# Edge convolution on one core: VectorE makes the comparison arrays of the next step behind the copy of column numbers instead of at the start of that step

## The chip, the cores and the metric

The kernel runs on one core of one Trainium2 chip. The metric is the device time of one execution in microseconds (us). The engines are TensorE (PE; its weight loads are shown apart as PEld), VectorE (DVE), ScalarE (ACT), GpSimd (POOL) and SyncE (SP), which only issues DMAs here. Each works through its own instructions in order, and they wait for each other by semaphores.

## The reference, cut to what matters

The whole block is a graph network layer over 6250 nodes and 100000 edges, an attention mixer and a mixture of experts. The change touches one stage, the edge convolution:

```python
# x[src]: 256 wide; edge_attr: 64 wide; dst is sorted
msg = jax.nn.relu(x[src] + edge_attr @ We + be)
aggr = jax.ops.segment_sum(msg, dst, num_segments=N)
z = (1.0 + GINE_EPS) * x + aggr
```

In the same stage the kernel also counts, for a later stage, how many of 131072 other edges end at each node. That count uses one-hot products too.

## The kernel before

`gine_windows` is the stage. The edges are cut into 98 steps (`S1`) of 8 blocks (`B`) of 128 edges. Buffers alternate by `q`, the parity of the step `k = 2i + q`, and a step has two halves `h` of four blocks. Since `dst` is sorted, the edges of a step end in a window of 128 nodes; `rel` holds each edge's place in the window. One step is made of:

- POOL, `gather` (L421): eight indirect DMAs of 128 rows of 256 numbers, `xg[q]`, by the column numbers in `gidx[q]`.
- SP (L400): one DMA of edge attributes `eaT[q]`.
- PE, `project` (L456): `ps_e[h] = eaT @ We`, four blocks in each half.
- DVE (L588), twice: `msg[q, h] = ps_e[h] + xg[q, h]`. ACT then does the relu in place (L506).
- DVE, the comparison arrays: `inwin[q]` (L576, one-hot of `rel` in the window), and for the count `hot_hi[q]` (L581) and `hot_lo[q]` (L583). All three compare with the numbers 0 to 127 in `ps_io`.
- PE: count products `ps_cnt += hot_lo.T @ hot_hi` (L463, eleven small bf16 products), and window sums `ps_a[q] = inwin.T @ msg` (L473, eight products).
- ACT, `save_sums` (L498): copies the sums of step k-1 to `nsum`. PE turns them (`turn_sums`, L444) in the middle of step k, and DVE adds the turned sums into `zT` (`add_window`, L569).
- DVE, `stage_next` (L562): copies the column numbers for step k+2 into `gidx[q]`, which starts POOL's next gather for that buffer. In even steps DVE also takes one `bn_stats` (L596).

PE's step k runs in this order: wait for `hot_lo[k]`, count (L463); wait for the first half of the messages of step k, project the first half of step k+1 (L456); wait for its relu, window sums of the first half (L473); turn the sums of step k-1 (L444); project the second half of step k+1; window sums of the second half. ACT's step k is: wait for the window sums of step k-1 and save them, then the two relus. DVE's step k before is: comparison arrays of step k, two message additions, column numbers, wait for turned sums (`s_nt`), `add_window`, `bn_stats`. The order on each engine is the order of the written code; no planner is involved.

In the print below, `s_am[q]` counts finished window sums, `s_cnt[q]` finished counts, `s_nt` turned sums, `s_sum` message halves, `s_e[q]` projected halves and `s_g[q][h]` gathered halves.

Of the kernel before, what the change touches and what calls it, by code (L numbers as in the profile page):

```python
# [13 lines left out]
ALU = mybir.AluOpType  # L14
# [12 lines left out]
B = 8  # L27
# [297 lines left out]
def gine_windows(nc, A, M):  # L325
# [5 lines left out]
    with ExitStack() as ctx:  # L331
# [59 lines left out]
        with nc.Block() as block:  # L391
# [122 lines left out]
            def _(dve):  # L514
# [43 lines left out]
                def stage_next(i, q):  # L558

                    for h in range(2):  # L560
                        dve.wait_ge(s_g[q][h], i * 64 + 64)
                    nc.vector.tensor_copy(gidx[:, q, :], M["src1"][:, bass.ds((i * 2 + q) * B + 2 * B, B)]).then_inc(s_gi, 1)  # L562

                def add_window(k, q):

                    at = nc.values_load(basei[0:1, k], engines=[dve.engine], min_val=0, max_val=N - 1,
                                        skip_runtime_bounds_check_because="VectorE clamped it to these bounds")
                    here = M["zT"][:, :, bass.ds(at, P)]
                    nc.vector.tensor_tensor(here, ps_a[:, q, D:2 * D].rearrange("p (c n) -> p c n", c=KD), here, ALU.add).then_inc(s_agg, 1)  # L569

                with dve.Fori(0, S1 // 2) as i:
                    for q in range(2):
                        k = 2 * i + q

                        dve.wait_ge(s_am[q], i + q)
                        nc.vector.tensor_tensor(inwin[:, q, :, :], ps_io[0:W1E, None, :].broadcast_to([W1E, B, P]),  # L576
                                                rel[:, bass.ds(k * B, B)][:, :, None].broadcast_to([W1E, B, P]), ALU.is_equal).then_inc(s_win[q], 1)

                        dve.wait_ge(s_cnt[q], i)
                        cols = bass.ds(k * CB, CB)  # L580
                        nc.vector.tensor_tensor(hot_hi[:, q, :, :], ps_io[:, None, 0:NHI].broadcast_to([P, CB, NHI]),  # L581
                                                M["hi"][:, cols][:, :, None].broadcast_to([P, CB, NHI]), ALU.is_equal).then_inc(s_hi, 1)
                        nc.vector.tensor_tensor(hot_lo[:, q, :, :], ps_io[:, None, :].broadcast_to([P, CB, P]),  # L583
                                                M["lo"][:, cols][:, :, None].broadcast_to([P, CB, P]), ALU.is_equal).then_inc(s_hot, 1)
                        for h in range(2):
                            dve.wait_ge(s_e[q], i * 2 + (h + 1))
                            dve.wait_ge(s_g[q][h], i * 64 + 64)
                            nc.vector.tensor_tensor(msg[:, q, h * HB:(h + 1) * HB, :].rearrange("p b d -> p (b d)"), ps_e[h][:, :],  # L588
                                                    xg[:, q, h * HB:(h + 1) * HB, :].rearrange("p b d -> p (b d)"), ALU.add).then_inc(s_sum, 1)
                        dve.wait_ge(s_sum, 2 * k + 2)  # L590
                        stage_next(i, q)
                        dve.wait_ge(s_nt, k + 1)
                        dve.wait_ge(s_agg, k)
                        add_window(bass.ds(k, 1), 1 - q)
                        if q == 0:
                            nc.vector.bn_stats(M["bst"][:, bass.ds(i, 1), :].rearrange("p t s -> p (t s)"),  # L596
                                               M["xn"][:, bass.ds(i, 1), :].rearrange("p t d -> p (t d)")).then_inc(s_stat, 1)
                dve.wait_ge(s_nt, S1 + 1)
                dve.wait_ge(s_agg, S1)
                add_window(slice(S1, S1 + 1), 1)  # L600
# [1874 lines left out]
```

## Time and profile before

| | us |
|---|---|
| median of 3 runs | 3788.47 (3782.95 to 3798.07) |
| the profiled execution, its own time | 3779.81 |
| its span, first to last instruction | 3777.8 |
| starts of `hot_lo` in the first and the last of the 98 steps | 81.7 and 1352.1 |

The profiled execution lies 8.7 us under the median. A line of the profile names the kernel's line, the engine, the operation, what it writes and reads, and behind the bar or in brackets how long the engine stood idle just before it and which instruction ended that. "remote" and "issue" mean that no instruction in the trace is seen to end the wait. One matrix product of f32 numbers is two records of the trace, so the four products of a half step are x8. A granted clock of 1.00 is 2.4 GHz and 0.50 is 1.2 GHz.

### The profile page before, as it was taken

The page shows a single profiled execution, that of the slowest core. Times are in us where ns is not written, and L with a number is a line of the kernel's source. Part 1 is how long each engine was busy: PE and PEld are TensorE (multiplying, and loading weights), DVE is VectorE, ACT ScalarE, POOL GpSimd, SP SyncE. Part 2 cuts the span into 40 slices and gives each one's busy share as a digit, 9 for nine tenths or more (in the row PEclk, how much of TensorE's full clock was granted, in tenths as well). Part 3 has the DMA queues.
Part 4 walks back from the last instruction along what each step waited for, and adds up shares of the span by engine and source line. Part 5 has one row for each costly group of instructions (what it writes and reads, how often), then busy time and mean ns, then how long its engine had stood idle before and what let it go on. Part 6 is the DMA issues. An engine that isn't in the chain of part 4 may idle for free. (4 is left out here: it accounts for less than half of the span.)

```text
span 3777.8 us, 34904 instructions
## 1 busy us (share of the span) xinstructions
PE 2708.7 (72%) x10528; PEld 1927.9 (51%) x10528; DVE 1621.8 (43%) x3135; ACT 692.7 (18%) x1082; POOL 1704.2 (45%) x1746
## 2 busy tenths in 40 slices
PE   3887888788788777799998865766766766765007
PEld 2666666666666655666665542433434433434006
DVE  6444555455454467666778960000000000001784
ACT  1111111111111123223332220111101101101005
POOL 1565656556565510022221216666666666662211
PEclk8777777777777779999999986878878877877558
DMA  7433333333333332200000013222222212213415
GB/s 259 131 105 91 106 101 106 99 100 104 97 108 93 99 99 74 68 23 23 23 23 12 9 12 70 37 36 37 37 36 37 37 31 37 41 30 109 145 59 229
DMA packets 215309, 280.82 MB, mean 74 GB/s; under 512 B 95634, under 2 KB 166312, under 8 KB 213706
## 3 DMA queue, kind: packets, MB, share of 16 engines
q0 software_dynamic: 68416, 133.35, 14.6%
q1 hardware_dynamic: 105994, 108.62, 9.3%
q10 hardware_dynamic: 40832, 38.01, 3.2%
q8 instruction: 35, 0.57, 0.1%
q14 instruction: 32, 0.26, 0.0%
HBM read 215.36 MB, written 64.48 MB: 74 GB/s over the span
## 5 line engine op out<-in xcount | busy, mean ns | idle before, releaser
L421 POOL DMA_INDIRECT xg<-xn_dram,gidx x784 | 743.9, 949 | 526.2 <-DVE gidx L562 283.2
L1962 POOL DMA_INDIRECT er<-row_dram,gi x784 | 739.9, 944 | 430.7 <-issue 411.9
L2023 PE MATMUL ps_en<-ew,hid 128*128 128x256 f32 x1568 | 404.5, 404 | 216.6 <-issue 213.4
L2095 DVE TENSOR_TENSOR eo<-ps_en,eb_r 128x1024 f32<-128x1024 f32 (+1 forms) x52 | 60.5, 1163 | 1157.7 <-remote 851.5
L2013 PE MATMUL ps_em<-zT_all,ew 128*128 (+2 forms) x832 | 420.4, 646 | 190.9 <-issue 123.7
L456 PE MATMUL ps_e<-we,eaT 65*128 65x256 f32 x1568 | 507.2, 480 | 69.3 <-issue 56.2
L473 PE MATMUL ps_a<-arena 128*128 128x256 f32 x1568 | 522.1, 491 | 34.6 <-ACT arena L506 26.4
L2023 PEld LDWEIGHTS ps_en<-ew,hid 128*128 128x128 f32 x1568 | 314.7, 202 | 311.6 <-issue 271.6
L473 PEld LDWEIGHTS ps_a<-arena 128*128 128x128 f32 x1568 | 399.0, 256 | 134.2 <-ACT arena L506 34.8
L456 PEld LDWEIGHTS ps_e<-we,eaT 65*128 65x128 f32 x1568 | 356.8, 239 | 138.8 <-issue 74.0
L2013 PEld LDWEIGHTS ps_em<-zT_all,ew 128*128 128x128 f32 x832 | 172.9, 215 | 419.6 <-issue 386.8
L2060 ACT ACTIVATE hid<-ps_em,eb 128x512 f32<-128x512 f32 (+1 forms) x208 | 130.4, 663 | 1087.2 <-DVE eo L2095 403.6
L569 DVE TENSOR_TENSOR zT_all<-ps_a,zT_all 128x256 f32 x99 | 42.1, 425 | 626.2 <-PE ps_a L444 358.5
L1514 POOL TENSOR_SCALAR hg<-hg,mv,rs 128x256 f32<-128x256 f32 x49 | 72.5, 1490 | 509.3 <-DVE rs L1320 462.7
L2268 PE MATMUL ps_c<-eo,dgm 128*128 128x256 f32 x294 | 69.4, 394 | 228.3 <-ACT dgm L2224 224.1
L588 DVE TENSOR_TENSOR arena<-ps_e,xg 128x1024 f32<-128x1024 f32 x196 | 230.0, 1216 | 0.0
L498 ACT ACTIVATE nsum<-ps_a 128x256 f32<-128x256 f32 x99 | 38.0, 384 | 1025.0 <-remote 792.0
L506 ACT ACTIVATE arena<-arena 128x1024 f32<-128x1024 f32 x196 | 198.5, 1049 | 49.9 <-DVE arena L588 30.0
L1613 PE MATMUL ps_m<-zT,arena 128*128 128x512 f32 (+1 forms) x416 | 183.8, 599 | 19.8 <-ACT zT L1682 19.4
L2268 PEld LDWEIGHTS ps_c<-eo,dgm 128*128 128x128 f32 x294 | 56.8, 197 | 240.9 <-issue 233.2
L1622 PE MATMUL ps_n<-arena,hid 128*128 128x256 f32 x784 | 173.9, 379 | 0.8 <-ACT hid L1688 0.8
L583 DVE TENSOR_TENSOR hot_lo<-ps_io,lo 128x1408 bf16<-128x1408 f32 x98 | 158.3, 1616 | 0.0
(291 smaller groups left out, 2877.0 us busy)
## 6 DMA issues: line engine op xcount, KB each, us to landing
eaT<-in_eaT SPq DMA_DIRECT2D x98, 256.0 KB
eo_dram<-eo ACTq DMA_DIRECT2D x48, 512.0 KB
eo<-eo_dram SPq DMA_DIRECT2D x12, 2048.0 KB
xg<-xn_dram,gidx POOLq DMA_INDIRECT x784
er<-row_dram,gi POOLq DMA_INDIRECT x784
xm<-xm_dram SPq DMA_DIRECT2D x24, 512.0 KB
erow<-arena ACTq DMA_DIRECT2D x1, 10240.0 KB
erow<-er SPq DMA_DIRECT2D x196, 40.0 KB
```

The lines of the kernel that those rows point to most:

```text
L421: pool.indirect_dma_start(xg[:, q, b, :], None, M["xn_dram"], bass.IndirectOffsetOnAxis(ap=gidx[:, q, b:b + 1], axis=0)).then_inc(s_g[q][b ...
L456: t = pe.matmul(ps_e[h][:, b * D:(b + 1) * D], eaT[:, q, h * HB + b, :], we[:, :], start=True, stop=True)
L473: t = pe.matmul(ps_a[:, q, 0:D], inwin[:, q, b, :], msg[:, q, b, :], start=(b == 0), stop=(b == B - 1), skip_group_check=True)
L506: nc.scalar.activation(msg[:, q, h * HB:(h + 1) * HB, :], msg[:, q, h * HB:(h + 1) * HB, :], ACT.Relu).then_inc(s_msg, 1)
L583: nc.vector.tensor_tensor(hot_lo[:, q, :, :], ps_io[:, None, :].broadcast_to([P, CB, P]), M["lo"][:, cols][:, :, None].broadcast_to([P, CB ...
L588: nc.vector.tensor_tensor(msg[:, q, h * HB:(h + 1) * HB, :].rearrange("p b d -> p (b d)"), ps_e[h][:, :], xg[:, q, h * HB:(h + 1) * HB, :] ...
L1613: m = pe.matmul(ps_m[c % 2][:, 0:w], mw1[:, k, c * P:(c + 1) * P], zT[:, k, 0:w], start=(k == 0), stop=(k == KD - 1))
L1622: m = pe.matmul(ps_n[:, t, :], hid[:, c, t * P:(t + 1) * P], mw2[:, c, :], start=(c == 0), stop=(c == KH - 1))
L1962: pool.indirect_dma_start(er[:, r, b, :], None, M["row_dram"], bass.IndirectOffsetOnAxis(ap=gi[:, r, b:b + 1], axis=0)).then_inc(s_get[r], 16)
L2013: m = pe.matmul(ps_m[c][:, 0:w], w1[:, e, k, c * P:(c + 1) * P], xT[:, k, at], start=(k == 0), stop=(k == KD - 1))
L2023: m = pe.matmul(ps_n[b][:, t, :], hid[:, b, c, t * P:(t + 1) * P], w2[:, e, c, :], start=(c == 0), stop=(c == KE - 1))
L2060: nc.scalar.activation(hid[:, b, c, 0:w], ps_m[c][:, 0:w], ACT.Gelu, bias=b1[:, e * KE + c:e * KE + c + 1]).then_inc(s_ge, 1)
```

## The change

The three comparisons become a function `compare(k, q, n)`. It is called once for step 0 ahead of the loop. Inside step k it is called for step k+1, with the other buffer, right behind `stage_next` and ahead of the wait for turned sums. To leave it out in the last step, the loop runs over `LASTI` (48) pairs, and the last two steps are written out behind it. The waits keep their meaning: `inwin` of step k+1 may be written once the window sums of step k-1 are done, and the `hot` arrays once the count of step k-1 is done. No instruction on another engine changes.

```diff
-                with dve.Fori(0, S1 // 2) as i:
+                def compare(k, q, n):
+
+                    dve.wait_ge(s_am[q], n + q)
+                    nc.vector.tensor_tensor(inwin[:, q, :, :], ps_io[0:W1E, None, :].broadcast_to([W1E, B, P]),
+                                            rel[:, bass.ds(k * B, B)][:, :, None].broadcast_to([W1E, B, P]), ALU.is_equal).then_inc(s_win[q], 1)
+
+                    dve.wait_ge(s_cnt[q], n)
...
+                def step(i, q, more):
+                    k = 2 * i + q
...
+                    dve.wait_ge(s_sum, 2 * k + 2)
+                    stage_next(i, q)
+                    if more:
+                        compare(k + 1, 1 - q, i + q)
+                    dve.wait_ge(s_nt, k + 1)
+                    dve.wait_ge(s_agg, k)
+                    add_window(bass.ds(k, 1), 1 - q)
...
+                compare(0, 0, 0)
+                with dve.Fori(0, LASTI) as i:
                     for q in range(2):
-                        dve.wait_ge(s_am[q], i + q)
...
-                        dve.wait_ge(s_sum, 2 * k + 2)
-                        stage_next(i, q)
-                        dve.wait_ge(s_nt, k + 1)
-                        dve.wait_ge(s_agg, k)
-                        add_window(bass.ds(k, 1), 1 - q)
...
+                        step(i, q, True)
+                step(LASTI, 0, True)
+                step(LASTI, 1, False)
```

On DVE, the second half of the loop's body (q = 1) reads as follows before. `arena<-ps_io,rel` is `inwin`, `arena<-ps_e,xg` a message half, and L566 is the wait for turned sums; `s_am11` is `s_am[1]`, `s_cnt11` is `s_cnt[1]`, and `s_e11` is `s_e[1]`.

```order
L576 ISA [waits s_am11]
L576 TENSOR_TENSOR arena<-ps_io,rel 128x1024
L581 ISA [waits s_cnt11]
L581 TENSOR_TENSOR hot_hi<-ps_io,hi 128x704
L583 REGISTER_ALU
L583 TENSOR_TENSOR hot_lo<-ps_io,lo 128x1408
L588 TENSOR_TENSOR arena<-ps_e,xg 128x1024 [waits s_std,s_e11]
L588 TENSOR_TENSOR arena<-ps_e,xg 128x1024 [waits s_xn,s_e11]
L590 ISA
L562 ISA [waits s_xn,s_std,s_sum1]
L562 COPY gidx<-src 128x8
L566 ISA [waits s_agg1,s_nt1]
```

Now the three comparisons for q = 1 stand in the first half of the body (q = 0), between the column numbers and the wait for turned sums (`s_nt1`, L566):

```order
L562 COPY gidx<-src 128x8
L573 REGISTER_ALU
L574 ISA [waits s_am11]
L574 TENSOR_TENSOR arena<-ps_io,rel 128x1024
L579 ISA [waits s_cnt11]
L579 TENSOR_TENSOR hot_hi<-ps_io,hi 128x704
L581 REGISTER_ALU
L581 TENSOR_TENSOR hot_lo<-ps_io,lo 128x1408
L566 ISA [waits s_agg1,s_nt1]
L566 TENSOR_LOAD basei
L569 ISA
L569 TENSOR_TENSOR zT_all<-ps_a,zT_all 128x2x128
```

The comparisons moved ahead of the addition L569. The message halves of q = 1 now follow the addition (and, in this half, `bn_stats`) directly; nothing was added to or taken from the body. L574, L579, L581 and L589 are the old L576, L581, L583 and L588.

## Rows read from the trace of the kernel before

**Rows 1.** The page: busy us (share of the span), instructions.

```profile
PE 2708.7 (72%) x10528; PEld 1927.9 (51%) x10528; DVE 1621.8 (43%) x3135; ACT 692.7 (18%) x1082; POOL 1704.2 (45%) x1746
```

**Rows 2.** The line of `hot_lo`: count, duration in ns, first and last start.

```profile
L583 DVE TENSOR_TENSOR hot_lo<-ps_io,lo x98: 1612/1616/1618, 81.7 to 1352.1; 128x1408 bf16<-128x1408 f32 x98
```

**Rows 3.** Groups by line over 82:1353: busy, mean ns | idle before, releasers.

```profile
L421 POOL DMA_INDIRECT xg<-xn_dram,gidx x773 | 731.0, 946 | 522.4 <-DVE gidx L562 283.2 <-issue 239.2
...
L456 PE MATMUL ps_e<-we,eaT 65*128 65x256 f32 x1552 | 500.0, 478 | 62.4 <-issue 56.2 <-DVE arena L588 6.2
...
L588 DVE TENSOR_TENSOR arena<-ps_e,xg 128x1024 f32<-128x1024 f32 x194 | 227.7, 1216 | 0.0
...
L463 PE MATMUL ps_cnt<-hot_hi,hot_lo 128*128 128x64 bf16 x1067 | 49.0, 196 | 131.9 <-DVE hot_lo L583 114.4 <-issue 17.5
```

**Rows 4.** Timeline of PE, one step: start, us, instruction, [idle before, releaser].

```profile
1003.11 3.56 PE L456 MATMUL ps_e<-we,eaT 65*128 65x256 f32 x8 [0.63 <-issue]
1006.47 3.62 PE L473 MATMUL ps_a<-arena 128*128 128x256 f32 x8
...
1010.25 1.89 PE L456 MATMUL ps_e<-we,eaT 65*128 65x256 f32 x8
1011.98 1.89 PE L473 MATMUL ps_a<-arena 128*128 128x256 f32 x8
1015.24 0.49 PE L463 MATMUL ps_cnt<-hot_hi,hot_lo 128*128 128x64 bf16 x11 [1.37 <-DVE hot_lo L583]
1016.37 3.18 PE L456 MATMUL ps_e<-we,eaT 65*128 65x256 f32 x8 [0.63 <-issue]
```

**Rows 5.** Timeline of DVE and ACT over the same step.

```profile
1004.34 0.17 DVE L562 COPY gidx<-src 128x8 int32 x1
1010.97 0.43 DVE L569 TENSOR_TENSOR zT_all<-ps_a,zT_all 128x256 f32 x1 [6.46 <-issue]
...
1011.65 1.21 DVE L576 TENSOR_TENSOR arena<-ps_io,rel 128x1024 f32<-128x1024 f32 x1
...
1013.57 1.62 DVE L583 TENSOR_TENSOR hot_lo<-ps_io,lo 128x1408 bf16<-128x1408 f32 x1
...
1016.70 0.39 ACT L498 ACTIVATE nsum<-ps_a 128x256 f32<-128x256 f32 x1 [10.77 <-remote]
1016.98 1.99 ACT L506 ACTIVATE arena<-arena 128x1024 f32<-128x1024 f32 x2
```

**Rows 6.** Windows: PE, PEld, DVE, ACT, POOL busy; granted clock, DMA share, GB/s.

```profile
82.00:1353.00 1271.00, 1043.71 (x4365) 817.58 (x4365) 634.16 (x729) 226.37 (x292) 731.40 (x774) 0.77 0.37 105
1003.40:1010.10 6.70, 6.70 (x18) 5.11 (x18) 0.96 (x2) 2.27 (x3) 3.78 (x4) 0.50 0.21 61
1010.20:1017.00 6.80, 4.80 (x32) 3.85 (x31) 6.03 (x7) 0.30 (x2) 3.79 (x4) 1.00 0.47 135
...
1770.00:1950.00 180.00, 170.22 (x753) 123.62 (x752) 131.34 (x367) 55.10 (x77) 43.10 (x24) 1.00 0.07 24
```

**Rows 7.** Timeline of POOL, where one gather follows the other without a wait.

```profile
961.36 0.94 POOL L421 DMA_INDIRECT xg<-xn_dram,gidx  x1 [1.86 <-DVE gidx L562]
...
971.36 0.95 POOL L421 DMA_INDIRECT xg<-xn_dram,gidx  x1 [0.30 <-issue]
```

**Rows 8.** Timeline of PE, a short step and the one behind it.

```profile
958.06 0.49 PE L463 MATMUL ps_cnt<-hot_hi,hot_lo 128*128 128x64 bf16 x11 [1.37 <-DVE hot_lo L583]
...
961.01 1.89 PE L473 MATMUL ps_a<-arena 128*128 128x256 f32 x8
...
967.82 0.49 PE L463 MATMUL ps_cnt<-hot_hi,hot_lo 128*128 128x64 bf16 x11 [1.23 <-DVE hot_lo L583]
...
978.55 0.70 PE L473 MATMUL ps_a<-arena 128*128 128x256 f32 x2 [0.34 <-issue]
...
989.15 0.77 PE L463 MATMUL ps_cnt<-hot_hi,hot_lo 128*128 128x64 bf16 x11 [4.18 <-DVE hot_lo L583]
```

**Rows 9.** The same view: the last such step.

```profile
1244.68 0.49 PE L463 MATMUL ps_cnt<-hot_hi,hot_lo 128*128 128x64 bf16 x11 [1.48 <-issue]
...
1265.45 0.49 PE L463 MATMUL ps_cnt<-hot_hi,hot_lo 128*128 128x64 bf16 x11 [2.60 <-DVE hot_lo L583]
```

More of the change, by code:

```diff
@@ L569, in add_window @@
                     nc.vector.tensor_tensor(here, ps_a[:, q, D:2 * D].rearrange("p (c n) -> p c n", c=KD), here, ALU.add).then_inc(s_agg, 1)
-                with dve.Fori(0, S1 // 2) as i:
-                    for q in range(2):
-                        k = 2 * i + q
-                        dve.wait_ge(s_am[q], i + q)
[L576 to L589, printed above, removed]
-                        dve.wait_ge(s_sum, 2 * k + 2)
-                        stage_next(i, q)
-                        dve.wait_ge(s_nt, k + 1)
-                        dve.wait_ge(s_agg, k)
-                        add_window(bass.ds(k, 1), 1 - q)
-                        if q == 0:
-                            nc.vector.bn_stats(M["bst"][:, bass.ds(i, 1), :].rearrange("p t s -> p (t s)"),
-                                               M["xn"][:, bass.ds(i, 1), :].rearrange("p t d -> p (t d)")).then_inc(s_stat, 1)
@@ new lines, in compare @@
+                def compare(k, q, n):
[3 more added lines that the diff above has]
+                    dve.wait_ge(s_cnt[q], n)
+                    cols = bass.ds(k * CB, CB)
+                    nc.vector.tensor_tensor(hot_hi[:, q, :, :], ps_io[:, None, 0:NHI].broadcast_to([P, CB, NHI]),
+                                            M["hi"][:, cols][:, :, None].broadcast_to([P, CB, NHI]), ALU.is_equal).then_inc(s_hi, 1)
+                    nc.vector.tensor_tensor(hot_lo[:, q, :, :], ps_io[:, None, :].broadcast_to([P, CB, P]),
+                                            M["lo"][:, cols][:, :, None].broadcast_to([P, CB, P]), ALU.is_equal).then_inc(s_hot, 1)
@@ new lines, in step @@
+                def step(i, q, more):
+                    k = 2 * i + q
+                    for h in range(2):
+                        dve.wait_ge(s_e[q], i * 2 + (h + 1))
+                        dve.wait_ge(s_g[q][h], i * 64 + 64)
+                        nc.vector.tensor_tensor(msg[:, q, h * HB:(h + 1) * HB, :].rearrange("p b d -> p (b d)"), ps_e[h][:, :],
+                                                xg[:, q, h * HB:(h + 1) * HB, :].rearrange("p b d -> p (b d)"), ALU.add).then_inc(s_sum, 1)
+                    dve.wait_ge(s_sum, 2 * k + 2)
[5 more added lines that the diff above has]
+                    add_window(bass.ds(k, 1), 1 - q)
+                    if q == 0:
+                        nc.vector.bn_stats(M["bst"][:, bass.ds(i, 1), :].rearrange("p t s -> p (t s)"),
+                                           M["xn"][:, bass.ds(i, 1), :].rearrange("p t d -> p (t d)")).then_inc(s_stat, 1)
```

## The prediction

> **What bounds the kernel now.** The page's shares say little: PE is busy 72% of the span and no engine is full [rows 1], because stages with different limits are added up. The change touches one stage, so I first fixed that stage by the line of `hot_lo`, which runs once per step: 98 starts from 81.7 to 1352.1 us [rows 2]. That is 1270.4 us for 97 intervals, 13.10 us a step. All that follows is made against this number; outside these 1270 us nothing changes.
>
> Then I read one step in the timeline of PE and asked where it stands still. From one count (L463) to the next there are only two holes: 1.37 us until VectorE's `hot_lo` is there, and 0.63 us between the count and the first projection [rows 4]. The second hole ends by nothing that the trace names, but the code says what it is: the projection waits for the first message half, and VectorE makes that half directly behind `hot_lo`. So both holes are one fact: VectorE starts the comparisons too late. The timeline of VectorE shows why. It finishes the column numbers at 1004.5, stands idle 6.46 us until the turned sums are there, adds them at 1010.97, and only then starts `inwin` at 1011.65, ending `hot_lo` at 1015.19 [rows 5]; PE starts the count 0.05 us later [rows 4]. VectorE is on the path for 3.5 us of comparisons that it could have made in its idle 6.46.
>
> Over the stage, the grouped lines give the same two holes: PE idle 131.9 us before L463 and 62.4 us before L456 [rows 3], together 194.3 us, or 2.0 us a step.
>
> Two more facts matter. The granted clock in the stage is 0.77 on average, and it alternates: 0.50 (1.2 GHz) from 1003.4 to 1010.1, where PE had come out of the two holes, then 1.00 (2.4 GHz) [rows 6]. Eight records take 3.4 us at the lower level and 1.7 us at the upper (1003.11 to 1006.47 against 1010.25 to 1011.98) [rows 4]. And POOL is not far away: where nothing holds it, eight gathers take 10.00 us (961.36 to 971.36, without a break between two groups) [rows 7].
>
> **The change part by part.**
>
> *Comparisons into the idle time.* VectorE's three comparisons cost 3.54 us from the start of the first to the end of the last (1011.65 to 1015.19) [rows 5]. They move into an idle stretch of 6.46 us, so in such a step they cost nothing there. Their own waits are for window sums and count of step k-1. The sums of the step before were seen by ScalarE at 1016.70, 2.8 us after PE's last product of them ended (1011.98 + 1.89 = 13.87) [rows 4, 5]. VectorE comes to them behind the column numbers, one step (13.26 us, from 1003.11 to 1016.37) after 1004.34, at 1017.6, so in this step that wait is over. If the cover were gone, the comparisons would delay `add_window` and the message halves behind it, at most by 3.54 us a step.
>
> *What is queued behind them.* On VectorE `add_window` and the next two message halves stand behind the comparisons. The column numbers stand ahead of them, so POOL's start is not delayed. ScalarE, SyncE and POOL keep their order.
>
> *What goes on PE.* `hot_lo` of step k+1 is ready a whole half step early, so the 1.37 us go. The first message half of step k+1 now comes right behind `add_window` (the comparisons themselves started 0.68 us behind its start, 1010.97 to 1011.65 [rows 5]), not behind 3.5 us of comparisons: with its 1.2 us (L588, mean 1216 ns [rows 3]) it is done 1.9 us after the addition starts, about 1012.9 by this step's times, while PE still works until 13.87. So the 0.63 us go as well. Term: 131.9 + 62.4 = 194.3 us [rows 3]. I take off 4 us for the first steps, where other things start up: 190 us.
>
> *What is late next.* ScalarE. Its relu of step k stands behind the copy of the sums of step k-1. Here copy and relu run from 1016.70; the first relu ends at 1016.98 + about 1.0 = 18.0 [rows 5]. PE's window sums of that step can't start before. If the sums are still seen 2.8 us late when PE no longer pauses, PE could start them at 18.0 instead of 19.35 (16.37 + 3.0), and the gain in this step is 1.3 us, not 2.0. In the step at full clock (958.06 to 967.82, 9.8 us) PE started its sums at 961.01 [rows 8], and nothing would be won. With three quarters of the steps like the first kind, this end is 0.75 x 97 x 1.3 = 95 us. These rows leave two reasons for the delay open: the sums may be seen late because PE pauses right behind them (then the delay goes with the pause), or for a reason of their own. The other groups of products, which PE follows up at once, let their readers start within 0.7 us (PE turned from turned sums to the projection at 1010.25, and `add_window` ran at 1010.97 [rows 4, 5]), so I lean to the first and keep 95 us as the low end.
>
> *The clock.* At the other end, if the holes are what lowers the clock, it stays up without them. In a stage without such holes, 1770 to 1950, PE is busy 170 of 180 us at 1.00 [rows 6]. Then PE needs 9.8 - 2.0 = 7.8 us a step and POOL becomes the bound at 10.0 us: POOL's whole wait for column numbers, 283.2 us [rows 3], goes and no more.
> The Trainium skill, TensorE: Matmul & The Clock Gate, section "A second HAM failure mode: psum-queue depth-cycling", says that short idles between groups of matmuls are enough to make the clock oscillate between half and full rate. The trace agrees in that the clock falls with holes of 1.37 and 0.63 us in the step and stays up where there are none. By that rule the time would be that of the POOL rival below.
> I don't take this end as the forecast: a PE that waits for POOL 2.2 us in 10.0 has a hole of the same size as now, and the clock would fall again.
>
> *Loop.* Two steps are written out behind the loop; the body has as many instructions as before. Nothing in the sum.
>
> **Sum.** Profiled execution 3779.8 - 190 = 3589.8. The median of the runs lies 8.7 us over the profiled execution, so 3598 us by the median. A step takes 13.10 - 1.96 = 11.1 us.
>
> **The rivals.**
>
> *POOL becomes the bound.* The clock rises, PE falls under 10.0 us a step, the gathers follow each other without a wait. Gain 283 us: 3505 us. For it: the holes and the clock go together [rows 4, 6], and gathers did run without a break [rows 7]. Against it: the new hole behind POOL.
>
> *The relu behind the copy.* The 95 us case above: 3693 us, steps of 12.1 us. For it: the copy is seen to wait 2.8 us after PE's last product. Against it: that product is one that PE pauses behind.
>
> *Slow stretches.* This one ends slower. From 978.55 on PE's products come with short unexplained idles where they otherwise follow each other every 0.22 us, and the step from 967.82 to 989.15 takes 21.3 us [rows 8]. It comes directly behind the short step of 9.8 us. There are six steps of 18.9 to 21.3 us in the stage, the last from 1244.68 to 1265.45 [rows 9], and five of them stand directly behind the only five steps under 10.3 us. If short steps bring on such a stretch (both PE and POOL are then at their densest), a kernel with steps of 10 us meets it again and again: two steps of 10.0 and one of 21.3 make 13.77 on average, 97 x 0.67 = 65 us slower: 3853 us. It decides from 13.1 us a step on; at 11 us a step that needs 25 more stretches of 8 us than now, every fourth step. Against it: most steps will not be as short as 10 us, and the dense stage at 1770 to 1950 runs at full rate with PE busier than here (but POOL and DMA nearly quiet, DMA share 0.07 against 0.37) [rows 6].
>
> *The change does not do what it says.* VectorE might reach the comparisons too late or be held in them by the late sums, so that `hot_lo` is no earlier. That needs the idle 6.46 us [rows 5] to be gone; at most the gain would be near nothing: 3788 us.
>
> **How the numbers follow.** Forecast (both holes go, the clock shares about as now, steps 10.7 to 11.5 us, 3560 to 3640 us): 0.37. POOL bound, or near it (3500 to 3560): 0.26. Relu behind the copy, or some more slow stretches that eat part of the gain (3640 to 3720): 0.25. Little left (3720 to 3769): 0.03. No change: 0.04. Slower: 0.05. The range reaches from the POOL end to most of the relu end: 3500 to 3700 us. A change of 0.5% is 19 us, about what a measurement of this kernel can tell from none. Faster by more than that 0.91, within it 0.04, slower 0.05.
>
> **What would show it.** Right: in the grouped lines PE's idle before L463 and before L456 falls from 194 us to under 20, the steps (98 starts of `hot_lo`) take about 11.1 us, VectorE's idle moves from before `add_window` to before the message halves or shrinks, and POOL's wait for column numbers falls by about the gain, to some 90 us. The POOL rival: that wait is near nothing, and steps are 10.0 us. The relu rival: PE's idle before L473, released by ScalarE's relu, grows from 24 us to 100. The slow-stretch rival: more than 20 steps above 18 us. The clock: under 0.77 or at it for the forecast, well above for the POOL rival. Wrong altogether would be an idle of PE before L463 that stays above 100 us.

## The result, and the profile after the change

The changed kernel takes 3864.19 us in the median of 4 runs (3841.99 to 3869.21), the kernel before 3791.55 us (4 runs, 3782.95 to 3798.07): a ratio of 1.0182, 95% interval 1.0143 to 1.022. The forecast was 3598 us with a range of 3500 to 3700. Both the number and the direction were wrong here; on another kind of chip, met later, the direction was right. The profiled execution of after is 3841.99 us, its span 3840.0.

First the line of `hot_lo`, as [rows 2], then the groups by line over 82:1420, as [rows 3] (busy us, mean ns | idle before, releasers), and the same stretch in the windows view, as [rows 6]:

```profile
L581 DVE TENSOR_TENSOR hot_lo<-ps_io,lo x98: 1615/1616/1617, 81.4 to 1412.6; 128x1408 bf16<-128x1408 f32 x98
```

```profile
L421 POOL DMA_INDIRECT xg<-xn_dram,gidx x773 | 730.9, 946 | 589.8 <-DVE gidx L562 358.8 <-issue 231.0
L473 PE MATMUL ps_a<-arena 128*128 128x256 f32 x1556 | 525.2, 481 | 234.8 <-issue 185.7 <-ACT arena L506 46.0
L456 PE MATMUL ps_e<-we,eaT 65*128 65x256 f32 x1552 | 448.8, 430 | 91.3 <-issue 52.0 <-DVE arena L589 38.5
...
L574 DVE TENSOR_TENSOR arena<-ps_io,rel 128x1024 f32<-128x1024 f32 x97 | 118.8, 1225 | 167.9 <-remote 150.0 <-issue 14.2 <-PE ps_a L473 3.4
...
L463 PE MATMUL ps_cnt<-hot_hi,hot_lo 128*128 128x64 bf16 x1078 | 59.2, 208 | 18.4 <-issue 16.5 <-DVE hot_lo L581 1.6
```

```profile
82.00:1420.00 1338.00, 994.06 (x4380) 765.43 (x4381) 644.27 (x732) 228.81 (x294) 731.29 (x774) 0.78 0.35 100
```

The stage grew from 1270.4 to 1331.2 us, 13.72 us a step. That is the whole loss of the profiled execution (62 us). The comparisons did what they should: PE's idle before the count fell from 131.9 to 18.4 us. But PE now stands 234.8 us before the window sums (L473). Before, that line read:

```profile
L473 PE MATMUL ps_a<-arena 128*128 128x256 f32 x1552 | 515.6, 490 | 32.8 <-ACT arena L506 24.5 <-issue 7.9
```

I split PE's idle in the stage by whether it stands ahead of the first product of a group or between two products of one group, which should follow each other without a gap:

| PE in the stage, us | before | after |
|---|---|---|
| ahead of a count (L463) or a projection (L456) | 131.9 + 60.5 | 3.9 + 44.6 |
| ahead of window sums (L473) | 25.8 | 167.9 |
| inside a group of products | 8.9 | 126.8 |
| busy | 1043.4 | 987.9 |

Each column adds up to the length of the stage. So the two holes lost 144 us, and as much (142) came back as one ahead of the window sums. On top come 118 us inside the groups, and PE's busy time fell by 55. The sum is the stage's 61 us.

The timeline of PE in one stretch shows both new losses (start, us, instruction, [idle before, releaser]):

```profile
556.14 1.89 PE L473 MATMUL ps_a<-arena 128*128 128x256 f32 x8
557.87 0.48 PE L463 MATMUL ps_cnt<-hot_hi,hot_lo 128*128 128x64 bf16 x11
558.19 1.97 PE L456 MATMUL ps_e<-we,eaT 65*128 65x256 f32 x8
565.27 3.78 PE L473 MATMUL ps_a<-arena 128*128 128x256 f32 x8 [5.11 <-issue]
...
590.24 0.38 PE L456 MATMUL ps_e<-we,eaT 65*128 65x256 f32 x1 [0.77 <-issue]
591.64 0.59 PE L456 MATMUL ps_e<-we,eaT 65*128 65x256 f32 x1 [1.03 <-issue]
...
593.06 0.58 PE L473 MATMUL ps_a<-arena 128*128 128x256 f32 x1 [0.40 <-issue]
594.46 1.22 PE L473 MATMUL ps_a<-arena 128*128 128x256 f32 x2 [0.82 <-issue]
...
599.41 0.59 PE L473 MATMUL ps_a<-arena 128*128 128x256 f32 x1 [0.82 <-issue]
600.12 0.77 PE L463 MATMUL ps_cnt<-hot_hi,hot_lo 128*128 128x64 bf16 x11
```

ScalarE and VectorE at the same places, in the same view:

```profile
563.89 0.38 ACT L498 ACTIVATE nsum<-ps_a 128x256 f32<-128x256 f32 x1 [14.24 <-remote]
564.17 1.99 ACT L506 ACTIVATE arena<-arena 128x1024 f32<-128x1024 f32 x2
```

```profile
558.16 0.17 DVE L562 COPY gidx<-src 128x8 int32 x1 [0.17 <-issue]
564.01 1.23 DVE L574 TENSOR_TENSOR arena<-ps_io,rel 128x1024 f32<-128x1024 f32 x1 [5.67 <-remote]
...
576.27 0.17 DVE L562 COPY gidx<-src 128x8 int32 x1
...
582.74 0.17 DVE L562 COPY gidx<-src 128x8 int32 x1 [0.17 <-issue]
```

**Late signals.** The window sums ended at 558.03 (556.14 + 1.89). ScalarE's copy and VectorE's `inwin` both wait for exactly these, and both start 5.9 us later, at 563.89 and 564.01. The relu stands behind the copy, so PE's next window sums stand still until 565.27. It is the signal that comes late and not its readers: of the 54 copies of after that start over 0.5 us late, 51 have an update of their semaphore in the trace, each time 0.02 us before the copy starts. (The profile models the ends of PE's products, so the last product itself may have ended later than 558.03.) And "issue" at 565.27 doesn't mean that PE waited for nothing: the relu ended at 565.22, but the trace has no record of its update of the semaphore, so the profile could not name it.

**Slow products.** From 590.24 on most of PE's records, or pairs of them, begin about 0.7 or 1.4 us apart (590.24, 591.64, 593.06, 594.46), where they begin 0.22 us apart otherwise at the full clock; it ends before 600.12. And POOL, which began its gathers again at 577.23:

```profile
568.42 0.95 POOL L421 DMA_INDIRECT xg<-xn_dram,gidx  x1 [0.30 <-issue]
577.23 0.94 POOL L421 DMA_INDIRECT xg<-xn_dram,gidx  x1 [7.86 <-DVE gidx L562]
...
595.99 0.95 POOL L421 DMA_INDIRECT xg<-xn_dram,gidx  x1 [0.30 <-issue]
604.94 0.94 POOL L421 DMA_INDIRECT xg<-xn_dram,gidx  x1 [8.00 <-DVE gidx L562]
```

Sixteen gathers run without a pause from 577.23 to 596.94, since the two copies of column numbers came only 6.47 us apart (576.27 and 582.74), less than eight gathers take. The slow products begin 13.0 us into this run and end some 2.5 us behind it. In before nearly all runs have eight gathers.

Steps by the starts of `hot_lo`: before has 7 over 18 us (one of them the first, at start-up) and 5 under 10.3; after has 21 over 18 (one of them at start-up) and 23 under 10.3, and 20 of those 23 are followed directly by one over 18.

### The profile page after: what moved, and what is told of

Read it like the earlier page. It is cut to its first block and busy times, and to the rows that moved or that the text cites. A ratio compares the mean times of both kernels' runs of the same rounds, so it can differ in the third digit from the quotient of the medians.

```text
span 3840.0 us, 34837 instructions
## 1 busy us (share of the span) xinstructions
PE 2653.0 (69%) x10528; PEld 1873.4 (49%) x10528; DVE 1629.4 (42%) x3135; ACT 692.1 (18%) x1082; POOL 1704.0 (44%) x1746
## 5 line engine op out<-in xcount | busy, mean ns | idle before, releaser
L421 POOL DMA_INDIRECT xg<-xn_dram,gidx x784 | 743.8, 949 | 593.6 <-DVE gidx L562 358.8
L473 PE MATMUL ps_a<-arena 128*128 128x256 f32 x1568 | 528.0, 480 | 234.8 <-issue 185.7
L2105 DVE TENSOR_TENSOR eo<-ps_en,eb_r 128x1024 f32<-128x1024 f32 (+1 forms) x52 | 60.5, 1163 | 1158.1 <-remote 938.3
L473 PEld LDWEIGHTS ps_a<-arena 128*128 128x128 f32 x1568 | 369.0, 240 | 368.1 <-issue 257.0
L456 PE MATMUL ps_e<-we,eaT 65*128 65x256 f32 x1568 | 456.0, 432 | 98.1 <-issue 52.0
L456 PEld LDWEIGHTS ps_e<-we,eaT 65*128 65x128 f32 x1568 | 323.2, 217 | 153.0 <-issue 67.0
L569 DVE TENSOR_TENSOR zT_all<-ps_a,zT_all 128x256 f32 x99 | 42.0, 424 | 501.1 <-remote 396.9
L589 DVE TENSOR_TENSOR arena<-ps_e,xg 128x1024 f32<-128x1024 f32 x196 | 230.6, 1216 | 13.5 <-remote 9.1
L574 DVE TENSOR_TENSOR arena<-ps_io,rel 128x1024 f32<-128x1024 f32 x98 | 120.0, 1225 | 167.9 <-remote 150.0
```

The costliest lines, as they stand in the source:

```text
L421: pool.indirect_dma_start(xg[:, q, b, :], None, M["xn_dram"], bass.IndirectOffsetOnAxis(ap=gidx[:, q, b:b + 1], axis=0)).then_inc(s_g[q][b ...
L456: t = pe.matmul(ps_e[h][:, b * D:(b + 1) * D], eaT[:, q, h * HB + b, :], we[:, :], start=True, stop=True)
L473: t = pe.matmul(ps_a[:, q, 0:D], inwin[:, q, b, :], msg[:, q, b, :], start=(b == 0), stop=(b == B - 1), skip_group_check=True)
```

## The experiments

A fact that came out between the experiments goes first, since every result hangs on it. **Chips differ.** On some chips the kernel before takes 3790 to 3800 us in the median; on others 3478 to 3490 us. On the first kind the profile has late signals and slow products, on the second it has neither, in any kernel. I call them the slower chips and the quicker chips; no chip is known to have been met twice, so whether this is the chip or its state at that time is open. Kernels are compared only with runs of before on the same chip.

The theories at the start: **A**, products that follow each other too densely make PE slow down; A1, what counts is the array's consumption, so zeros would help; A2, what counts is the rate of PE's instructions. **B**, gathers without a pause hold PE up. Later: **C**, the change is good by itself, and the loss comes from the slower chips; **D**, the new order on VectorE costs on any chip.

### Taking one load away: no gathers, zeros, half the sums

All three start from the changed kernel. Without gathers:

```diff
-                    for b in range(B):
-                        pool.indirect_dma_start(xg[:, q, b, :], None, M["xn_dram"],
-                                                bass.IndirectOffsetOnAxis(ap=gidx[:, q, b:b + 1], axis=0)).then_inc(s_g[q][b // HB], 16)
...
+                c.done(nc.vector.memset(xg[:, :, :, :], 0.5))
```

> The changed kernel without its 784 gathers in the edge convolution: xg is filled once with 0.5, VectorE waits for no gather, GpSimd only passes semaphores on; the sums are not the reference's. In the changed kernel 97 steps take 1331 us (13.7 us a step), with some 25 steps over 18 us in which TensorE's products come at 0.7 us and more apart. Theory A (TensorE itself: products without a pause at the full clock bring on the slow stretches): the slow stretches stay, since TensorE is as dense or denser, and steps stay well above 10 us on average, the whole at 3700 to 3850 us. Theory B (gathers that follow each other without a break, or their transfers, bring them on): no step over 15 us is left, TensorE bounds the stage at 7.8 to 8.5 us a step, and the whole takes 3791 - 97 x (13.1 - 8.2), about 3320 us.

Zeros in PE's products:

```diff
-                sp.dma_start(we[0:ED, :], A["We"]).then_inc(s_w, 16)
-                sp.dma_start(we[ED:ED + 1, :], mm(A["be"], 1)).then_inc(s_w, 16)
...
+                nc.vector.memset(we[:, :], 0.0).then_inc(s_w, 1)
...
-                                                xg[:, q, h * HB:(h + 1) * HB, :].rearrange("p b d -> p (b d)"), ALU.add).then_inc(s_sum, 1)
+                                                xg[:, q, h * HB:(h + 1) * HB, :].rearrange("p b d -> p (b d)"), ALU.mult).then_inc(s_sum, 1)
```

> The changed kernel with the same instructions and waits, but zeros run through TensorE in the edge convolution: the weights of the projection are zeroed instead of loaded, and the messages are ps_e times xg instead of ps_e plus xg, so all f32 products move zeros; the sums are not the reference's. Theory A1 (it is what the array consumes at full rate with real numbers, so the operands matter): no slow stretch is left, steps are 10.0 us, bound by the gathers, the stage takes about 980 us and the whole about 3864 - 350 = 3510 us. Theory A2 (it is the rate of TensorE's instructions, whatever they compute) and theory B (the gathers): nothing changes, the stage stays at 1331 us and the whole at 3840 to 3870 us.

Two window-sum products in each half instead of four:

```diff
-                        for b in range(h * HB, h * HB + HB):
+                        for b in range(h * HB, h * HB + 2):
```

> The changed kernel with half of the window sums left out: two products instead of four in each half step, all other work and all transfers as before; the sums are not the reference's. TensorE has 24 f32 records a step instead of 32, 5.8 us of work a step at the full clock. Theory A (TensorE's density): the slow stretches go or become rare (under 5), steps are near the gathers' 10.0 us and the stage near 1000 us, the whole about 3530 us. Theory B (gathers without a break): with steps of 10.0 us the gathers run without a break all the time, so there are as many slow stretches as in the changed kernel or more, the stage stays over 1250 us and the whole over 3790 us.

Measured: 3033.08, 3263.3 and 3261.36 us, where before takes 3477.96 on the same chip, with steps of 7.56, 10.01 and 10.00 us. It looked as if each of the three cured the stage. But in the stage of experts, which none of them touches, TensorE's products had also shrunk from 1196 us to some 699, so the chip was another one, and the experiments told nothing of the cause. What they do give is a bound. Without gathers PE alone needs 7.56 us a step at full clock:

```profile
L577 DVE TENSOR_TENSOR hot_lo<-ps_io,lo x98: 1611/1615/1617, 85.8 to 819.5; 128x1408 bf16<-128x1408 f32 x98
```

```profile
86.00:819.00 733.00, 730.04 (x4337) 635.03 (x4338) 638.46 (x726) 219.54 (x291) 0.00 (x0) 0.99 0.14 40
```

That is the line of `hot_lo` and the windows view of the repeat on a second quicker chip (3028.61 us, before 3490.12).

### The same kernels on a slower chip, and half of the change

> The changed kernel itself, beside the kernel before on the same chip. Where the kernel before takes about 3480 us (as it did beside the three runs without slow stretches) and not 3790 us, the slow stretches belong to the chip and not to the program. Theory C (the change is good by itself, and only a chip with slow stretches turns it into a loss): on a chip where before takes about 3480 us, the changed kernel has no step over 15 us, steps of 10.0 us bound by the gathers, and takes about 3265 us, ratio 0.94; on a chip where before takes about 3790 us, ratio 1.018 again with some 25 steps over 18 us. Theory D (the loss is in the order on VectorE, whatever the chip): the ratio is 1.00 or above on either chip.

> The kernel before, for its trace on the same chip. Theory C: on a chip that takes 3480 us for it, no step over 15 us in the edge convolution, steps of 12 to 13 us with the two holes of 1.37 and 0.63 us on TensorE, and none of the stretches in the expert stage in which products come at 0.7 us and more apart. If the chip takes 3790 us for it: some 6 steps over 18 us, as in the first trace. Theory D: TensorE's holes are the same on either chip.

The changed kernel repeats: 3843.34 us against 3799.03, ratio 1.013 (1.0064 to 1.0196), steps of 13.73 us, though only 15 of them are over 18 us and 20 under 10.3; before in one run 3800.89 us, 13.24 us a step. Two kernels make half of the change. One makes the `hot` arrays early and leaves `inwin` behind the addition, the other the reverse:

```diff
                     if more:
-                        compare(k + 1, 1 - q, i + q)
+                        counts(k + 1, 1 - q, i + q)
...
+                    if more:
+                        windows(k + 1, 1 - q, i + q)
```

> Half of the change: the two hot arrays of the count are made early, as in the changed kernel; inwin (1.1 us) is made behind the addition of turned sums, as before. TensorE's count then waits for nothing, but the first projection waits for the message half, which comes 1.1 us later than in the changed kernel. On a chip without slow stretches theory C expects steps between 10.0 and 10.5 us and 3265 to 3310 us. On a chip with them: TensorE pauses about 1 us a step, so there are fewer stretches than in the changed kernel (10 to 18 instead of 25), steps of 12.8 to 13.4 us and 3760 to 3830 us. Theory D: within 10 us of the changed kernel on either chip.

> The other half: inwin is made early, the two hot arrays (2.4 us) behind the addition, as before. TensorE's hole before the count shrinks from 1.37 to about 0.25 us and the 0.63 us behind it stay. On a chip without slow stretches theory C expects steps of 10.0 to 11.5 us and 3270 to 3400 us; on a chip with them about 12.5 to 13.2 us a step, 5 to 15 stretches and 3740 to 3800 us. Theory D: within 10 us of the changed kernel on either chip.

Measured: 3880.39 us, ratio 1.0236 (1.0167 to 1.0305), steps of 14.01 us; and 3862.34 us, ratio 1.0168 (1.0102 to 1.0235), 14.05 us in the profiled execution. Neither half is better than the whole, and both forecasts were missed: 22 and 30 steps over 18 us (with the start-up) instead of 10 to 18 and 5 to 15. With `inwin` late, PE waits 127.9 us for the message halves behind it; with the `hot` arrays late, PE's wait for them is back, at 170.4 us. But the slow products are in both. The loss does not belong to one of the three comparisons.

### Repeats that met quicker chips, and the comparison they made possible

The three kernels above ran again, and a version with less work for PE. It writes the relu's output and `inwin` in bf16, so that a window-sum product is one record instead of two:

```diff
-        inwin = M["arena"][0:W1E, 2 * B * D:2 * B * (D + P)].rearrange("p (q b n) -> p q b n", q=2, b=B)
+        inwin = M["arena"][0:W1E, 2 * B * D:2 * B * D + B * P].bitcast(BF16).rearrange("p (q b n) -> p q b n", q=2, b=B)
...
-                            t = pe.matmul(ps_a[:, q, 0:D], inwin[:, q, b, :], msg[:, q, b, :], start=(b == 0), stop=(b == B - 1), skip_group_check=True)
+                            t = pe.matmul(ps_a[:, q, 0:D], inwin[:, q, b, :], msg16(q, h)[:, b - h * HB, :], start=(b == 0), stop=(b == B - 1), skip_group_check=True)
...
-                            nc.scalar.activation(msg[:, q, h * HB:(h + 1) * HB, :], msg[:, q, h * HB:(h + 1) * HB, :], ACT.Relu).then_inc(s_msg, 1)
+                            nc.scalar.activation(msg16(q, h), msg[:, q, h * HB:(h + 1) * HB, :], ACT.Relu).then_inc(s_msg, 1)
```

> The kernel without gathers again (the changed kernel, xg filled once with 0.5, GpSimd passes semaphores on only), since the first time it ran on a chip that shows no slow stretch in any stage and so told nothing about their cause. On a chip where the kernel before takes about 3790 us: theory A (TensorE's own density brings on the stretches) expects TensorE to work almost without a pause and so to meet them more than ever, the stage at 1000 us or above against 733 us on the quiet chip. Theory B (gathers) expects steps of 7.6 us and no step over 12 us, the stage 733 us as on the quiet chip. On a quiet chip: again 733 us.

> The changed kernel, with the window sums in bf16: inwin is written as bf16 (zeros and ones, exact) and ScalarE's relu writes its result as bf16; all sums stay in f32. Eight short products take the place of sixteen f32 records a step, so TensorE's f32 work a step falls from 7.8 us at the full clock to about 4.5. This is the candidate that should beat both kernels if TensorE's density is what brings on the stretches. Theory A: no or under 5 steps over 18 us, steps of 10.0 us bound by the gathers, the stage at about 975 us on either chip; the whole at 3480 to 3520 us where before takes 3790, ratio 0.92 to 0.93, and at 3265 us where before takes 3480. Theory B (gathers without a break bring them on): the stage stays over 1250 us where before takes 3790, ratio 0.99 to 1.02.

These and the repeats of zeros and half sums (3259.72 and 3258.39 us) met a quicker chip: bf16 sums take 3257.92 us there, ratio 0.9344 (0.9292 to 0.9395), at 9.99 us a step. A second set brought what was missing, the changed kernel itself on a quicker chip:

> The changed kernel once more. Theory C on a chip where before takes about 3480 us: steps of 10.0 us, no step over 15 us but the first, the whole at 3265 us, ratio 0.94. On a chip where before takes about 3790 us: ratio 1.01 to 1.02 and 15 to 25 steps over 18 us, as twice before. Theory D (the order on VectorE costs time on any chip): a ratio of 1.00 or above on the quiet chip too.

> The kernel whose f32 products in this stage move zeros. If the chip shows slow stretches (before about 3790 us): theory A1 (consumption of the array) expects none of them in this stage and the stage at 971 us; theory A2 (rate of instructions) and theory B (gathers) expect it near 1331 us. On a quiet chip 971 us.

> The changed kernel with the window sums in bf16. If the chip shows slow stretches: theory A expects the stage at 975 to 1050 us and a ratio of 0.92 to 0.93; theory B the stage over 1250 us and a ratio of 0.99 to 1.02. On a quiet chip 3258 us and a ratio of 0.934, as before.

The changed kernel takes 3264.58 us where before takes 3490.14: **ratio 0.9357 (0.9297 to 0.9417)**. C stands, D falls. Zeros take 3263.12, half sums 3261.99, bf16 sums 3259.07 us (ratio 0.9341): all the same, because POOL is the bound. The line of `hot_lo` of the changed kernel there, the windows of the stage and of the experts, and the groups by line:

```profile
L581 DVE TENSOR_TENSOR hot_lo<-ps_io,lo x98: 1611/1615/1616, 81.8 to 1052.9; 128x1408 bf16<-128x1408 f32 x98
```

```profile
82.00:1053.00 971.00, 831.50 (x4354) 677.34 (x4355) 637.85 (x727) 239.42 (x291) 727.88 (x772) 0.93 0.49 138
1979.00:2678.00 699.00, 684.04 (x2399) 453.88 (x2400) 60.04 (x51) 135.48 (x208) 528.27 (x560) 0.99 0.30 58
```

```profile
L421 POOL DMA_INDIRECT xg<-xn_dram,gidx x771 | 729.0, 946 | 237.4 <-issue 226.2 <-DVE gidx L562 11.2
L456 PE MATMUL ps_e<-we,eaT 65*128 65x256 f32 x1549 | 405.3, 407 | 114.4 <-DVE arena L589 113.6
L473 PE MATMUL ps_a<-arena 128*128 128x256 f32 x1544 | 401.2, 406 | 11.1 <-ACT arena L506 11.1
L589 DVE TENSOR_TENSOR arena<-ps_e,xg 128x1024 f32<-128x1024 f32 x194 | 235.8, 1217 | 296.0 <-DMA xg<-xn_dram,gidx 295.4
L463 PE MATMUL ps_cnt<-hot_hi,hot_lo 128*128 128x64 bf16 x1067 | 47.9, 194 | 14.2 <-DVE hot_lo L581 11.6
```

10.01 us a step: POOL waits 11.2 us for column numbers in the whole stage, VectorE waits 295.4 us for gathered rows. Some 760 gathers run here without a pause, and no product is slow. Signals are prompt. The sums end at 607.43 and the copy starts at 607.47, in the timelines of PE and ACT:

```profile
605.54 1.89 PE L473 MATMUL ps_a<-arena 128*128 128x256 f32 x8
```

```profile
607.47 0.38 ACT L498 ACTIVATE nsum<-ps_a 128x256 f32<-128x256 f32 x1 [5.44 <-PE ps_a L473]
```

### Zeros and bf16 sums on a slower chip

> The kernel whose f32 products in this stage move zeros. If the chip shows slow stretches (before about 3790 us): theory A1 (what the array consumes) expects none of them in this stage and the stage at 971 us; theory A2 (rate of instructions) and theory B (gathers) expect it near 1331 us with 15 to 25 steps over 18 us. On a quiet chip 971 us.

> The changed kernel with the window sums in bf16. If the chip shows slow stretches: theory A (TensorE's density) expects the stage at 975 to 1050 us and a ratio of 0.92 to 0.93; theory B (gathers without a break) the stage over 1250 us and a ratio of 0.99 to 1.02. On a quiet chip a ratio of 0.934.

> The kernel before, for its trace. On a quiet chip: TensorE's holes of 1.37 and 0.63 us a step as in the first trace, no step over 15 us but the first, steps of 12.3 to 12.7 us (13.10 less the six slow stretches of about 8 us each over 97 steps) and the expert stage near 700 us against 1196 us. If theory C is wrong in that the quiet chip differs in more than the stretches, the steps are shorter than 12 us. On a chip with slow stretches: as in the first trace.

This time the chip was a slower one: before takes 3798.46 us (and 3796.44 in the single run whose trace was kept). Zeros: 3852.97 us, 13.69 us a step, 18 of its 22 steps under 10.3 us followed by one over 18. What PE multiplies doesn't matter; A1 falls. bf16 sums: 3834.77 us, ratio 1.0089 (1.0054 to 1.0125), 13.62 us a step. In this kernel the granted clock is 0.50 all through the stage:

```profile
82.00:1402.00 1320.00, 974.82 (x3567) 727.90 (x3568) 643.82 (x726) 230.30 (x291) 733.22 (x774) 0.50 0.35 101
```

PE starts 3567 records in 1320 us, 2.7 per us, against 4365 in 1271 us, 3.4 per us, in before [rows 6]; each runs at half the clock. PE is busy 74% of the stage instead of 82%. It is less dense than before on average, and still it alternates between steps of 8.8 and 18.7 us. Within its short steps it starts 37 records in 8.8 us, 4.2 per us. PE keeps the same rate for 180 us in the stage from 1770 to 1950 (753 records [rows 6]), on the slower chip and without slow products; POOL is nearly quiet there. So the rate of PE's instructions alone doesn't bring on the slow products, and A2 falls. On a quicker chip the same kernel, also at 0.50, has steps of 9.99 us. The timeline of PE in one of the long steps, and POOL's gathers around it:

```profile
616.00 0.72 PE L467 MATMUL ps_cnt<-hot_hi,hot_lo 128*128 128x64 bf16 x8
617.18 0.21 PE L467 MATMUL ps_cnt<-hot_hi,hot_lo 128*128 128x64 bf16 x1 [0.46 <-issue]
619.28 0.27 PE L467 MATMUL ps_cnt<-hot_hi,hot_lo 128*128 128x64 bf16 x2 [1.88 <-issue]
624.64 3.78 PE L460 MATMUL ps_e<-we,eaT 65*128 65x256 f32 x8 [5.10 <-DVE arena L593]
```

```profile
599.36 0.95 POOL L425 DMA_INDIRECT xg<-xn_dram,gidx  x1 [7.75 <-DVE gidx L566]
...
618.55 0.95 POOL L425 DMA_INDIRECT xg<-xn_dram,gidx  x1 [0.30 <-issue]
626.82 0.94 POOL L425 DMA_INDIRECT xg<-xn_dram,gidx  x1 [7.32 <-DVE gidx L566]
```

Sixteen gathers from 599.36 to 619.50, PE slow from some 17 us into them.

### What the traces say of B

Three counts over the traces bear on B. The first is on **late signals**: the time from the end of the last window-sum product before each of ScalarE's copies to the start of that copy (about 95 copies in each trace), split by whether POOL had started a gather in the last 1.3 us before that end.

| | chip | POOL gathering: copies, seen over 0.5 us late | POOL not gathering: copies, late | all delays together, us |
|---|---|---|---|---|
| before | slower | 88, 80 | 6, 0 | 239 |
| after | slower | 51, 48 | 43, 5 | 223 |
| zeros | slower | 50, 41 | 44, 13 | 182 |
| bf16 sums | slower | 94, 47 | 0 | 297 |
| after | quicker | 94, 0 | 0 | 4 |
| bf16 sums | quicker | 94, 0 | 0 | 4 |

Where the run of gathers was over 6 us old at that end, 75 of 76 sums are seen late in before and 35 of 35 in after, with medians of 2.82 and 4.93 us. The delays did not grow by the change (239 and 223 us in all). The exceptions are not few: of the sums that ended while POOL was not gathering, 9 of 46 are late in the repeat of after and 12 of 28 in the kernel with the `hot` arrays early, and with bf16 sums half of those under gathers are on time.

The second is on **runs of gathers**. In before and its two repeats on slower chips, 5, 5 and 6 runs have twelve gathers or more without a pause (of 0.9 us or more), and 15 of the 22 steps over 15 us stand on one of them; in after there are 43 such runs, and 41 of 42 long steps stand on one. Of the other steps 18 of 266 stand on one in the three traces of before, but 49 of 55 in after, so the count says something for before and little for after. In the kernel with the `hot` arrays early only 22 of 43 long steps stand on such a run. The seven others of before stand on two groups parted by a pause of about 1.8 us, the one of after is at start-up. With pauses under 2.3 us not counted as one, every long step in all nine traces from slower chips stands on such a run (249 of 249), but so do 540 of the 620 others, so this says little.

The third count is by **stage**: the lengths of four parts of the changed kernel on either kind of chip, and how many semaphore updates the trace has in them:

| part of the changed kernel | slower: us, updates | quicker: us, updates |
|---|---|---|
| edge convolution, first gather to last turned sums | 1358.0, 5347 | 999.8, 16051 |
| from there to the first gather of the experts | 905.0, 3944 | 904.8, 3944 |
| experts, to the first of the last 49 gathers | 1219.7, 4602 | 996.7, 20875 |
| the rest | 291.3, 1735 | 291.8, 1740 |

The two kinds of chip differ only in the two parts in which POOL issues 784 gathers each. That speaks for B. But the same two parts show a rival that no run tests. On the slower chip the trace lacks two thirds of the updates of the edge convolution (346 of the engines' 1644 and the rest of the DMAs'), on the quicker one none of the engines'. So what writes the trace falls behind exactly there, and it may be this writing, and not the gathers as such, that holds up TensorE and its signals. Every execution on record comes with a span and a granted clock, so no time here is known to be free of it.

So both losses appear mostly while POOL's gathers go on, and only on slower chips. The direct tests, the kernel without gathers on a slower chip and a time taken without the recording, were not made. That the stages with gathers bring the losses on a slower chip is supported; which part of it is the cause is not shown.

No version beat both kernels on a slower chip. On a quicker one the changed kernel and bf16 sums are alike.

## Why the prediction was wrong

**The stage and its two holes: right.** 1270 us, two holes that are one fact, and VectorE's comparisons as their cause. The change emptied the hole before the count (131.9 to 18.4 us). For the two together I had named "under 20"; they kept 109.7, of which 48.5 lies ahead of a group of products and the rest inside one. POOL's wait for column numbers, forecast at some 90 us, rose from 283.2 to 358.8.

**The comparisons in VectorE's idle time: right on a quicker chip, wrong on a slower one.** I took the late sums of one step (2.8 us) and found that VectorE comes to them later still. On the quicker chip VectorE waits 1.8 us in all before L574. On the slower chip it waits 167.9 us there, because the same signal comes up to 11.9 us late (up to 9.7 in before, where VectorE came to it later).

**What is late next: the right chain, the wrong size and the wrong reading.** I saw that ScalarE's copy waits 2.8 us after PE's last product, and that the relu and the window sums hang on it. I left two reasons open and leaned to "because PE pauses behind it". The timeline of after answers it: PE doesn't pause behind 558.03, and the delay is 5.9 us. It goes with the chip, and mostly with the gathers. The delays are as long in all as in before (223 and 239 us); there they ran beside the holes, and without the holes nothing covered them. So this end was no low end with 95 us of gain. PE's idle ahead of the window sums rose by 142 us, and ate the 144 that the holes gave up. This is the first step that failed.

**Slow stretches: the mechanism that I priced and gave 0.05.** 13.77 us a step and 3853 us were forecast for it, 13.72 us and 3864 us were measured; "more than 20 steps above 18 us" came as 21, one of them at start-up, and as 15 in the repeat. That the number fits so well is partly luck: the rival's sum has only slow stretches in it, while the loss is made of 118 us inside the groups, 142 us ahead of the sums, and the 144 us and 55 us that came off, and the steps are not two of 10.0 and one of 21.3 (23 of 97 are under 10.3, 42 over 15). The second step that failed is the weighing. I argued that such stretches need steps of 10 us, and that most steps would be longer. But in before they come mostly with POOL's gathers in long runs, and my own forecast would have made these: at 11.1 us a step and eight gathers in 10.0 [rows 7], POOL pauses 1.1 us a step, and in before pauses of 1.8 us already had long steps behind them. In before nearly all runs were of eight gathers, in after 43 have twelve or more. [rows 8] and [rows 9] showed that five of six long steps follow the five shortest (in the two repeats of before it is 2 of 8 and 4 of 8); I named the coupling (PE and POOL both at their densest) and didn't ask which of the two it was. What I put against the rival, the dense stage from 1770 to 1950 at full rate, was dense for PE alone, with POOL nearly quiet [rows 6]. It spoke against PE alone as the cause and for what goes with the gathers.

**The decision point** (13.1 us a step) was the arithmetic of a mean, but short steps bring their own long ones here: a group of steps under 10 us puts POOL behind, POOL catches up with sixteen gathers, and the step that stands on their end takes 18 to 20 us. That is the order in which the traces show it; the cause behind it is not shown.

**The clock: wrong.** I held against the POOL rival that a hole behind POOL would lower the clock again. On the quicker chip PE waits 114.4 us before the projections, and the granted clock of the stage is 0.93; over the whole execution it rose there from 0.83 in before to 0.88. On the slower chip it stayed at 0.77 in the stage, where PE's idle did not shrink but grew. The rule of the Trainium skill that I had weighed and set aside (TensorE: Matmul & The Clock Gate, "A second HAM failure mode: psum-queue depth-cycling": short idles between groups of matmuls make the clock oscillate) agrees with the direction on the quicker chip. It is no complete account, since bf16 sums hold the clock at 0.50 on both kinds of chip, with PE busy 975 of 1320 us on the slower and 947 of 968 us on the quicker one.

**POOL as the bound: right on quicker chips.** 10.01 us a step for 10.0 in that rival, and a wait of POOL for column numbers of 11.2 us (283.2 in before on a slower chip). The total gain there is 226 us (3490.14 to 3264.58), not 283. No trace of before on a quicker chip exists; if all else is alike, its stage took 971 + 226 = 1197 us, 12.3 us a step.

## What to carry to other kernels

A wait that the profile ends by "remote" or "issue" and that is longer than its fellows is a fact to settle first: here the same sums were seen 0.04 us late in some places and 2.8 us in others, and what made the difference decided the sign of the change. It also pays to count the updates of semaphores in the trace: where they are missing, "remote" and "issue" hide a releaser. When a stall is taken from one engine, ask which other engine's bursts it had been keeping apart, and look in the trace before for the few places where those bursts already touch: their steps are a sample of the kernel after. And a stage that the edit doesn't touch should be read in every result, since its length tells whether the chip is the same.

## What the runs showed of the hardware that was not expected

- Chips differ by 9% for the kernel before, 3478 to 3490 against 3790 to 3800 us, and by 18% for the changed one. TensorE's products of the experts' stage, untouched by the change, take 699 us at a granted clock of 0.99 on one and 1196 us at 0.79 on the other. The whole stage takes 997 and 1220 us, since on the quicker chip the gathers go on for 271 us behind the products. The row of the slower chip:

```profile
2336.00:3532.00 1196.00, 805.78 (x2398) 486.70 (x2399) 60.05 (x51) 129.52 (x208) 734.40 (x779) 0.79 0.21 38
```

- On the slower chips TensorE's products come in stretches about 0.7 or 1.4 us apart, even small bf16 products of which eleven take 0.49 us otherwise [rows 4], and its finished sums are seen up to 11.9 us late, mostly while POOL issues indirect gathers. The instructions of VectorE and POOL take as long as on the quicker ones (1216 ns for a message half, 946 ns for a gather). What PE's instructions and signals share with the gathers or with the recording of their landings, and why only on some chips, stays open.
- On the slower chips the traces lack most of the semaphore updates of the two stages with gathers, and none of those of the part between them (the table by stage).
- The granted clock of the bf16 kernel is 0.50 through the whole stage on both kinds of chip.
- An indirect gather of 128 rows of 1 KB takes POOL 0.95 us and 0.30 to the next, 1.25 us together, alike on all chips.
